# MLP and half of V made by halves of rows in pairs of tiles, single score units between the pieces, transposed scores behind the MLP

## What is computed

```python
x = L0_attn_query
xn = _layernorm(x, axis=-1)
s = _L0_attn_ref(xn, key, value, Wqkv, Wproj, bproj)   # 16 heads of 16, attention within each sequence of 256
g = _silu(_L0_ffn_ref(xn, proj1, proj1_bias, proj2, proj2_bias, gate_w))
x = x + s * g
```

```python
attn = jnp.einsum('gqd,gkd->gqk', q, k) * norm
attn = jax.nn.softmax(attn, axis=-1)
ctx = jnp.einsum('gqk,gkd->gqd', attn, v)
...
h = jax.nn.gelu(jnp.einsum('lne,he->lnh', x, proj1) + proj1_bias, approximate=False)
out = jnp.einsum('lnh,eh->lne', h, proj2) + proj2_bias
```

## Time and profile before

| | |
|---|---|
| median of 3 runs | 120.58 us (120.48 to 120.94) |
| the profiled execution | 120.94 us, its span 119.2 us |
| busy TensorE (PE), its weight loads (PEld) | 113.9 us, 88.5 us |
| busy VectorE (DVE), ScalarE (ACT), GpSimd (POOL) | 84.2, 74.2, 71.0 us |
| first F1 matmul, first S unit | 23.88 us, 29.42 us |
| last S unit, first PV matmul | 71.40 to 72.06 us, 81.17 us |

### The profile page before, as it was taken

How to read it: one execution, slowest core, us unless ns; L and a number is a source line. 1 busy time by engine, 2 the same in 40 slices (tenths; PEclk the granted TensorE clock), 3 DMA queues, 4 the chain that set the end, 5 groups by cost and what they waited for, 6 DMA issues and landing times.

```text
span 119.2 us, 2560 instructions
## 1 busy us (share of the span) xinstructions
PE 113.9 (96%) x930; PEld 88.5 (74%) x930; DVE 84.2 (71%) x158; ACT 74.2 (62%) x109; POOL 71.0 (60%) x92
## 2 busy tenths in 40 slices
PE   6989999999999999999999999999999999999980
PEld 5589998887878988888768777776775867566660
DVE  0789994530997889989899498305855838998861
ACT  4064696469978302331296979899868888799000
POOL 4227679009999904777979759699604341517471
PEclk9999999999999999999999999999999999999999
DMA  3999945555665455310000004400000000020213
GB/s 127 292 343 391 321 140 202 180 200 202 204 208 199 130 195 204 104 30 10 7 12 4 0 0 173 186 7 8 11 0 0 0 6 0 9 85 2 86 56 123
DMA packets 9633, 13.27 MB, mean 111 GB/s; under 512 B 2453, under 2 KB 4885, under 8 KB 9493
## 3 DMA queue, kind: packets, MB, share of 16 engines
q1 hardware_dynamic: 9332, 12.85, 32.2%
q10 hardware_dynamic: 288, 0.26, 0.7%
HBM read 5.51 MB, written 1.05 MB: 55 GB/s over the span
## 4 chain that ended last, share of the span: by engine, by line
PE 90%; DMA 4%; ACT 1%; DVE 1%; SPq 1%; issue 0%
PE bank L799 39%; PE bank L908 14%; PE bank L925 12%; PE bank L889 9%; PE bank L875 8%; PE bank L905 6%; DMA wqkv_raw<-wqkv 4%; PE bank L936 1%; PE bank L832 1%; SPq L327 1%; ACT wqh L511 1%; DVE bank L768 0%; DVE fin L779 0%; ACT xTh L520 0%
## 5 line engine op out<-in xcount | busy, mean ns | idle before, releaser
L688 DVE TENSOR_REDUCE negm<-bank 128x4 f32<-128x1024 f32 x32 | 37.3, 1216 | 9.9 <-PE bank L875 9.9
L452 POOL TENSOR_TENSOR hTl<-hG,hTh 128x512 fp32r<-128x512 f32 x16 | 20.4, 1293 | 8.7 <-ACT hTh L565 8.3
L908 PE MATMUL bank<-w2s,hTh 128*128 128x512 f32 x64 | 23.7, 410 | 0.0
L576 ACT ACTIVATE PT<-bank 128x1024 f32<-128x1024 f32 x16 | 15.4, 1026 | 2.8 <-PE bank L889 2.7
L905 PE MATMUL bank<-w2s,hTl 128*128 128x256 f32 x64 | 16.6, 280 | 0.0
L908 PEld LDWEIGHTS bank<-w2s,hTh 128*128 128x128 f32 x64 | 11.7, 188 | 3.1
L561 ACT ACTIVATE hG<-bank,b1s 128x512 f32<-128x512 f32 x16 | 10.9, 682 | 3.5 <-PE bank L799 3.4
L905 PEld LDWEIGHTS bank<-w2s,hTl 128*128 128x128 f32 x64 | 12.1, 188 | 0.5
L889 PEld LDWEIGHTS bank<-qs,ks 50*128 50x128 f32 x128 | 8.4, 185 | 3.8 <-issue 1.4
L889 PE MATMUL bank<-qs,ks 50*128 50x256 f32 x128 | 11.0, 299 | 0.0
L875 PEld LDWEIGHTS bank<-ks,qs 48*128 48x128 f32 x128 | 8.3, 185 | 3.2 <-issue 2.8
(11 more groups left out here) (96 smaller groups left out, 228.7 us busy)
## 6 DMA issues: line engine op xcount, KB each, us to landing
qs<-stage SPq DMA_DIRECT2D x24, 128.0 KB, 2.8
ks<-stage SPq DMA_DIRECT2D x24, 128.0 KB, 2.8
xs<-x SPq DMA_DIRECT2D x4, 256.0 KB, 4.6
w_raw<-w SPq DMA_DIRECT2D x1, 1024.0 KB, 7.9
w_in_place<-w SPq DMA_DIRECT2D x1, 1024.0 KB, 10.6
xb<-x SPq DMA_DIRECT2D x1, 1024.0 KB, 5.7
wqkv_raw<-wqkv SPq DMA_DIRECT2D x3, 256.0 KB, 5.3
out<-fin SPq DMA_DIRECT2D x6, 128.0 KB, 1.7
```

The lines of the kernel that those rows point to most:

```text
L452: nc.gpsimd.tensor_tensor(hTl[:, n % FC, :], hG[:, n % FC, :], hTh[:, n % FC, :].bitcast(f32), ALU.subtract).then_inc(h_lo, 1)
L576: nc.scalar.activation(exp_of(w), scores_of(*s), ACT.Exp).then_inc(exp_done, 1)
L688: nc.vector.tensor_reduce(negm[:, j, :, s[1] % 2, b, :], scores_of(*s), axis=AX.X, op=ALU.max, negate=True).then_inc(max_done, 1)
L908: m = nc.tensor.matmul(bank_of("F2", u, 0), hTh[:, fc, c:c + P], w2s[:, fc].rearrange("p a e -> p (a e)"), start=fc == 0, stop=fc == FC - 1)
```

## The change

- **Pairs by halves of rows.** Two tiles of F1 (`R1`), the two of the second half of V (`RV`), or two early tiles of F2 (`R2`) are made together. Each full matmul is cut into two of 64 rows. In the first turn the upper half of the rows makes the first tile's share and the lower half the second tile's, into their two banks; in the second turn the halves change over. TensorE waits between the turns until all matmuls of the first are done (`turn_made`). Both tiles are finished only at the end of the second turn.
- **Single score units.** `S_PLAN` lists the pairs and behind which of their pieces one score unit stands: 32 units, none in a group. S units now take two pairs of banks (0 to 3), F1, V and F2 four banks (4 to 7).
- **ST behind the MLP.** The first three ST units follow the last S unit and the last pair at once. They take bank pairs 0-1, 2-3 and 6-7; the late F2, PV and PJ use 4 and 5. F2 of tiles 4 and 5 is cut in other places. Late F2 stays on 128 rows.
- **Moved.** The DMAs of ones stand between the halves of the stacking; the maxima rows of the first group are issued by ScalarE's queue behind V instead of by SP's. The high and low parts of w2 are made ahead of all GELUs and `hTl`s. wph is made ahead of the second half of F1. The early gates are cut in sum and gate, those of tiles 2 and 3 come behind the last `hTl`; tanh and gate steps have places of their own in the list. The order of the first S units is another.

```diff
+BEHIND = {("RV", 0): [("MROWS",)], ("R1", 5): [("TANH", 2), ("TANH", 3)]}
+
+PARTS = {"R1": 2, "RV": 2, "R2": 4}
+
+MID = {2: [("TANH", 0)], 4: [("TANH", 1)]}
+
+S_PLAN = [("R1", 0, (3,)), ("R1", 1, (1, 2, 3)), ("R1", 2, (1, 3)), ("R1", 3, (1, 2, 3)), ("RV", 0, (1, 3)),
+          ("R2", 0, (0, 2, 3, 5, 6)), ("R2", 1, (0, 1, 3, 5, 7)), ("R1", 4, (1, 2, 3)), ("R1", 5, (1, 3)),
+          ("R1", 6, (1, 2, 3)), ("R1", 7, (1, 2, 3))]
...
-PAIRS = ([(j, b) for half in range(2) for j in range(2) for b in (2 * half, 2 * half + 1)]
+PAIRS = ([(0, 0), (0, 1), (1, 0), (0, 2), (0, 3), (1, 1), (1, 2), (1, 3)]
...
+def members(kind, p, *part):
+
+    if kind == "RV":
+        return [("V", 1, 0), ("V", 1, 1)]
+    return [({"R1": "F1", "R2": "F2"}[kind], n) + (part if kind == "R2" else ()) for n in (2 * p, 2 * p + 1)]
+
+
+def pieces(kind, p):
+
+    return [(kind, p, turn, part) for turn in range(2) for part in range(PARTS[kind])]
...
-    filler = [("F1", n) for n in range(FC)] + [("V", 1, p) for p in range(2)]
-    filler += ffn[:4 * TT // 2] + [("F1", n) for n in range(FC, 2 * FC)]
     units = [("S", w) for w in range(2 * GROUPS)]
-    for ahead in (4, 2, 3, 3, 4, 4, 4, 3, 2, 3, 2):
-        order += [filler.pop(0) for _ in range(ahead)] + [units.pop(0) for _ in range(min(3, len(units)))]
-    assert not filler and not units
...
+    for kind, p, behind in S_PLAN:
+        for n, piece in enumerate(pieces(kind, p)):
+            order.append(piece)
+            if n in behind:
+                order.append(units.pop(0))
+            if (kind, p) == ("R2", 1):
+                order += MID.get(n, [])
+        order += members(kind, p, 3) + BEHIND.get((kind, p), [])
+    assert not units
...
-    order += f2(4, 0, 1) + st(0) + f2(4, 2, 3) + f2(5, 0) + st(1) + f2(5, 1, 2, 3) + st(2) + pv(0, 1, 2)
-    order += st(3) + [("TURN", 0, 0)] + f2(6, 0, 1, 2, 3) + st(4) + pv(3, 4, 5)
...
+    order += st(0) + f2(4, 0, 1, 2) + f2(5, 0) + st(1) + f2(5, 1, 2) + f2(4, 3) + f2(5, 3)
+    order += st(2) + [("TANH", 4), ("TANH", 5)] + bias(0, 1) + pv(0, 1, 2) + [("GATE", 4), ("GATE", 5)]
...
-                    home[s] = (2 * (s[1] % 3), 2 * (s[1] % 3) + 1)
+                    home[s] = (2 * (s[1] % 2), 2 * (s[1] % 2) + 1)
                 elif kind == "ST":
-
-                    home[s] = (2 * ((s[1] + 2) % 3), 2 * ((s[1] + 2) % 3) + 1)
+                    home[s] = ((0, 1), (2, 3), (6, 7))[s[1] % 3]
...
-                    home[s] = (4 + turn % 4,) if n < first_f1 else (6 + turn % 2,)
+                    home[s] = (4 + turn % 4,)
...
+                if q == 1:
+
+                    sp.wait_ge(ones_ready, 1)
+                    for par in range(2):
+                        sp.dma_start(ks[64 * par + STK:64 * par + STM, :, :].bitcast(f32)
+                                     .rearrange("p h (b t) -> p (h b) t", t=SQ),
+                                     ones[0:2, None, :].to_broadcast([2, HP * B, SQ])).then_inc(ones_rows, 16)
...
-                if n in (3, 4):
-                    pool.wait_ge(w2_hi, n - 2)
-                    fs = slice(4 * (n - 3), 4 * (n - 3) + 4)
-                    nc.gpsimd.tensor_tensor(w2s[:, fs, 1, :], w2_in_place[:, fs, 1, :], w2s[:, fs, 0, :].bitcast(f32),
-                                            ALU.subtract).then_inc(w2_lo, 1)
...
-                    early_gate(0)
-                    early_gate(1)
                     split_maxima(0)
-                    early_gate(2)
+                    for u in range(2):
+                        early_sum(u)
...
+            for u in range(2, 4):
+                early_gate(u)
...
+                elif s[0] == "MROWS":
+                    maxima_rows(act, act, 0)
+                elif s[0] == "TANH" and s[1] < EARLY:
+                    u = s[1]
+                    act.wait_ge(yh_pool, u + 1)
+                    if u >= 2:
+                        act.wait_ge(gate_part, u - 1)
+                    nc.scalar.activation(th[:, u % 2, :], sums_of(u)[:, 0], ACT.Tanh).then_inc(th_done, 1)
...
+                elif s[0] in PARTS:
+                    kind, p, turn, part = s
+                    both = members(kind, p, 0)
+                    if (turn, part) == (0, 0):
+                        for one in both:
+                            wait_free(one)
+                    if (turn, part) == (1, 0):
+
+                        n_turn += 2
+                        pe.wait_ge(turn_made, n_turn)
+                    first, end = (turn, part) == (0, 0), part == PARTS[kind] - 1
+                    if kind == "R1":
+                        pe.wait_ge(w1_hi, 2)
+                        todo = [(kc, a, b) for a, b in ((0, 0), (1, 0), (0, 1)) for kc in range(KC)]
+                        todo = todo[3 * part:3 * part + 3]
+                        if part == 0:
+                            pe.wait_ge(w1_lo, 1)
+                        if part == 1:
+                            pe.wait_ge(w1_lo, 2)
+                        made = f1_made
+                    elif kind == "RV":
+                        todo = [(kc, a, b) for a, b in ((0, 0), (1, 0), (0, 1)) for kc in range(KC)]
+                        made = v_made
+                    else:
+                        pe.wait_ge(h_lo, FC * (p // 2) + 2 * part + 2)
+                        pe.wait_ge(w2_lo, 2)
+
+                        todo = [(fc, low) for fc in (2 * part, 2 * part + 1)
+                                for low in ((0, 1) if fc < FC - 1 else (1, 0))]
+                        made = f2_made
+                    for n, item in enumerate(todo):
+                        for half in range(2):
+                            one = both[turn ^ half]
+                            rows = slice(64 * half, 64 * half + 64)
+                            if kind == "R1":
+                                kc, a, b = item
+                                h, f = divmod(one[1], FC)
+                                dst = bank_of(*one)
+                                lhs = (w1h, w1l)[a][rows, kc, f * P:(f + 1) * P]
+                                rhs = (xTh, xTl)[b][rows, kc, h * HALF:(h + 1) * HALF]
+                            elif kind == "RV":
+                                kc, a, b = item
+                                c = (4 + 2 * one[2] + part) * P
+                                dst = bank_of(*one)[:, part * E:(part + 1) * E]
+                                lhs = (xTh, xTl)[a][rows, kc, c:c + P]
+                                rhs = (wqh, wql)[b][rows, 2, kc, :]
+                            else:
+                                fc, low = item
+                                c = (one[1] % 4) * P
+                                dst = bank_of(*one)[:, 0:E] if low else bank_of(*one)
+                                lhs = (hTh, hTl)[low][rows, fc, c:c + P]
+                                rhs = w2s[rows, fc, 0, :] if low else w2s[rows, fc].rearrange("p a e -> p (a e)")
+                            done = end and n == len(todo) - 1
+                            m = nc.tensor.matmul(dst, lhs, rhs, start=first and n == 0, stop=done and turn == 1)
+                            if done:
+                                m.then_inc(made if turn == 1 else turn_made, 1)```

TensorE, from the first F1 tile on. In these rows `xTh`, `w1h` and their low parts make F1, `ks,qs` is an S unit, and x12 is the number of matmuls in a row. Before:

```order
L799 MATMUL bank<-xTh,w1h 128x512 x2
L799 MATMUL bank<-xTh,w1l 128x512 x2
L799 MATMUL bank<-xTl,w1h 128x512 x2
L875 MATMUL bank<-ks,qs 128x256 x12
L799 MATMUL bank<-xTh,w1h 128x512 x2
L799 MATMUL bank<-xTh,w1l 128x512 x2
L799 MATMUL bank<-xTl,w1h 128x512 x2
```

More of the change, by code:

```diff
@@ L255, in banks @@
                 free[s] = list(dict.fromkeys(w for k in home[s] for who, w in taken.get(k, ()) if who != beside))
-                whole = not late or kind == "PV" or s[2] == (KC - 1 if kind == "PJ" else 3)
+                whole = s[2] == KC - 1 if kind == "PJ" else s[2] == 3 if kind == "F2" and late else True
                 if whole:
@@ L317, in by_rows, with maxima_rows @@
             return cd[:, n, :].rearrange("p (c r) -> p c r", r=32)
+        def maxima_rows(engine, queue, j):
+            engine.wait_ge(m_hi, j + 1)
+            engine.wait_ge(m_lo, j + 1)
+            for m in range(4):
+                for part in range(2):
+                    rows = qs[STK + part:P:64, 2 * j:2 * j + 2, :].rearrange("a h (g t) -> a (h g) t", t=P)
+                    queue.dma_start(rows[:, :, 32 * m:32 * m + 32].bitcast(f32),
+                                    mm[32 * m:32 * m + 32, j, part, :].bitcast(f32)).then_inc(m_rows[j], 16)
         block = ctx.enter_context(nc.Block())
@@ L495, in _ @@
                     nc.gpsimd.tensor_tensor(fin[:, u % 4, :], fin[:, u % 4, :], xb[:, u, :], ALU.add).then_inc(fin_pool, 1)
[L497 to L500 removed]
+                if s[0] == "BIAS":
+                    add_bias(s[1])
         @block.scalar
```

133 lines of the change are left out of this document (57 added, 76 removed), and 10 rows, old and new, of the table SPOTS.

## The result

The changed kernel took 121.49 us (median of 20 runs, 120.50 to 124.65) against 120.53 us for the kernel before (20 runs, 120.36 to 121.10). The ratio is 1.0046, 95% interval 1.0032 to 1.0060: slower by a little, where I forecast 120.5 and no change. The ratio leaves out the executions over 1.5% above the fastest, of which the changed kernel has seven; by the medians it is 1.0080. So there are two things to explain: a lowest time that is hardly higher (120.50 against 120.36), and executions that lie up to 4 us above it.

A forecast was written before the change was run, and what follows sets the result against it. TensorE, busy 113.9 of 119.2 us, was taken to bound the kernel. The terms -4.0 - 0.17 + 1.1 + 0.7 + 2.3 gave -0.1 us, so a median of 120.5 us, range 118.8 to 122.2.

The forecast's parts named there:

- Mode changes removed, 4.0 us: Up to the last score unit, 20 changes between 128 rows and half rows go, at 0.2 us each: -4.0 us.
- the paces: In MLP and V, a pair of half-row matmuls takes 0.230 us like a full one, a score unit 0.233: no cost.
- The rival of 0.24 per pair: Half-row pairs accumulating in two banks run at 0.24 us, +1.3 us or more: slower, 122.1 us; chance 0.23.
- the two far ones: 48 and 64 rows are two modes, 133 us; or loads can't overlap their own half's matmuls, 140; chance 0.03 each.
- The turn: Between a pair's turns PE waits for its own matmuls: 0.08 us with a unit between, 0.31 for the first; +1.1 us.
- Unit 8: With two score buffers, this score unit waits for VectorE's reduces behind the 1.28 us scaling of b2s: +0.7 us.
- the sum had -2.4: Up to the last score unit's end: terms -4.0, -0.17 (a bank wait gone), +1.1 and +0.7 us.
- The join, +2.3: From last score unit to first PV, waits for reduces and exponentials add 2.7 us, one pair of row changes saves 0.4.
- Behind the PV of the first groups the work is the same in other banks.: After the first PV groups, to the end of the kernel, nothing was to change: no cost.
- These land at 47.72 + 1.91 + 2.8 = 52.4: The second half of the stacks, behind the ones rows, lands at 52.4 us, delayed by their 1.91 us of SP.
- Unit 20 ... comes at ... 55.3: PE reaches the score unit that needs those stacks at 55.3 us, after they land at 52.4: no wait.
- What moves and costs nothing: Moved ones rows, maxima DMAs, w2 split, GpSimd's gates and the work behind the first PV groups were costed at nothing.

The follow-up runs named there:

- units_off_turns: Changed kernel with the score units between the two turns of a pair moved one or two pieces away: 123.02 us, ratio 1.0197 to the kernel before.
- act_delay: Changed kernel with one more 512-column ScalarE copy ahead of the table load: 121.88 us, ratio 1.0090 to the kernel before.
- f2_ahead: Changed kernel with two parts of F2 of tile 4 ahead of the first transposed units: 121.94 us, ratio 1.0098 to the kernel before.
- before_join: Kernel before with only the first three transposed units moved right behind the last score unit: 121.92 us, ratio 1.0108 to the unedited one.
- best_ones_early: Changed kernel with F2 of tiles 4 and 5 in the join's gaps and earlier GpSimd bias steps, ones rows still ahead: 121.09 us, ratio 0.9982.
- bias_early: Changed kernel with GpSimd's bias steps of tiles 2 to 6 about one group earlier: 121.01 us, ratio 1.0020 to the kernel before.
- ones_last: Changed kernel with the two ones-row DMAs behind all stacks again: 120.85 us, ratio 1.0027 to the kernel before.
- best: Changed kernel with ones rows behind all stacks, F2 of tiles 4 and 5 in the join's gaps, and earlier GpSimd bias steps: 120.09 us, ratio 0.9961.
- before_ones_early: Kernel before with only the ones rows moved ahead of the second half of the stacks: 121.39 us, ratio 1.0041 to the unedited one.
- join_full: Changed kernel with F2 of tiles 4 and 5 put in the gaps of the join: 120.61 us, ratio 0.9995 to the kernel before.

## Why the prediction was wrong

Point by point, by its own steps.

- *Mode changes removed, 4.0 us, and the paces.* Right in kind: no loss around units, pieces at 0.46 to 0.47 us for two pairs. The rival of 0.24 per pair fell, and so did the two far ones. A unit takes 0.24 to 0.25, not 0.233: 0.3 us over 32. By the Trainium skill's rule on loads, "TensorE: Matmul & The Clock Gate", Part 3, under what overlaps and what doesn't, each pair would also have shown its load; the trace doesn't agree, at 0.23 per pair.
- *The turn.* 0.12 for a covered one, 0.35 for the first, against 0.08 and 0.31: +0.4 us. That a waiting load starts late was right (units_off_turns).
- *Unit 8.* No wait. The scaling of b2s took 0.28 us, not the 1.28 of the earlier trace rows: -0.7. With the 0.2 at unit 20 these make -2.1 us for the stage where the sum had -2.4; measured are -2.17. That this term of the sum came out so well is in part luck: +0.7 for units and turns and -0.7 for unit 8 cancel.
- *The join, +2.3.* Measured +2.1, with the waits where I had them. ScalarE's chain sets its end: delaying it moves the end by as much (act_delay), and taking away the waits for the reduces gains nothing (f2_ahead). before_join shows those waits in the old kernel.
- *"Behind the PV of the first groups the work is the same in other banks."* Wrong, +0.4 us, and by the profiles the larger of the two misses. I looked at PE's instructions and not at which of VectorE's now run beside GpSimd's.
- *"These land at 47.72 + 1.91 + 2.8 = 52.4", "Unit 20 ... comes at ... 55.3".* Wrong too. I took the 1.91 us of issue for the price of the ones rows. The last stack was issued 3.0 us later than I had it (52.6 instead of 49.6), and PE came to unit 20 at 54.7, 0.6 earlier, mostly because unit 8 had no wait. So the 2.9 us of slack became a wait that cost 0.2 to 0.3 us in the profiled execution, 1.6 in the profile of act_delay and 2.0 in that of best_ones_early (without what half a clock added there).

The last two stand in one paragraph of the prediction, *"What moves and costs nothing"*, and this is the step that failed: I costed both moves at nothing and gave no price for the case that the cover of the stacks is gone. By the ratios they are the difference: bias_early and ones_last take 0.27 and 0.20% from 0.46%, which leaves the kernel before, and so the forecast. No run has just these two together, but best, which has them with the other join, is as much faster as the three parts add up to. The median is higher still than this ratio, because the wait at unit 20 differs between executions and can be followed by half a clock, as in best_ones_early. Of the changed kernel itself no such execution was profiled.

The rows of the kernel before had the price of the ones rows, and I had not looked there. Windows: first the kernel before behind its last stack, where the two transfers run with nothing behind them until 54 us; then the stretch from 32 to 38 us, first in the kernel before and last in before_ones_early:

```profile
49.00:54.00 5.00, 5.00 (x36) 4.17 (x35) 4.55 (x6) 1.62 (x3) 4.08 (x8) 1.00 0.14 29
32.00:38.00 6.00, 6.00 (x38) 4.80 (x38) 6.00 (x6) 5.08 (x8) 6.00 (x4) 1.00 0.59 202
32.00:38.00 6.00, 6.00 (x42) 4.79 (x40) 5.41 (x5) 5.06 (x9) 6.00 (x5) 1.00 0.23 61
```

The DMA engines move 29 GB/s at a busy share of 0.14 for the 5 us behind the stacks, where stacks run at 202 and 0.59. At 29 GB/s the 128 KB of the two take 4.5 us, an estimate from these rows. Moved ahead, they take the rate among the stacks down from 202 to 61 GB/s.

What stays open: why these two transfers run so slowly, why the landing of the last stack differs (3.0, 3.5 and 3.8 us at most), and what decides whether a wait is followed by a fall of the clock. act_delay waited 1.4 us at unit 20 at a clock of 1.00 throughout. ones_last has two runs at a mean clock of 0.986 that are only 0.6 us longer, and join_full has one of 123.84 us, 3.6 above its lowest, at a clock of 1.00. I know of no trace that tells these apart.

## What to carry to other kernels

Price a DMA that is moved ahead of others by how long its transfer keeps the DMA engines at a low rate, not by its own time of issue, and give the slack of each that waits behind it. When work is moved on one engine, list what the others now run at the same time: a saving of 2 us on PE was given back in three places, of which only the wait at unit 20 lies in the stage that was changed. A wait of PE that differs between executions shows in the spread before it shows in one profile, so look at all times and clocks and not at the profiled one alone.
